# The four corners of a deformable-convolution tile: two additions of halves in one buffer instead of one strided reduction

## The reference

```
x = x + L0(gn(x))     # 7x7 neighbourhood attention
x = x + L1(gn(x))     # 3x3 convolution
x = x + L2(gn(x))     # deformable 3x3 convolution
x = x + L3(gn(x))     # two Mamba passes over the pixels
```

```
sampled = v00*(1-wy)*(1-wx) + v01*(1-wy)*wx + v10*wy*(1-wx) + v11*wy*wx
sampled = sampled * mask
out = einsum('bkhwc,ock->bohw', sampled, w2)
```

## Time and profile before

| | |
|---|---|
| two executions | 6243.54 and 6252.93 us, median 6248.24 us |
| the profiled execution | span 6244.6 us, 55481 instructions |
| from the span's start to the first gather, loading, L0 and the first image's L1 | 885.6 us |
| first gather to the last addition of `stage_flow` | 885.6 to 3134.5 us |
| rest (normalisation and Mamba) | 3134.5 to 6244.6 us |
| VectorE busy | 5012.8 us (80% of the span) |
| GpSimd busy | 4904.1 us (79%) |
| TensorE busy | 4411.3 us (71%) |

### The profile page before, as it was taken

One profiled execution on the slowest core, in us unless ns is written; L12 is line 12 of the kernel. 1 busy time (PEld: TensorE's weight loads), 2 busy tenths in 40 slices (PEclk: granted clock), 3 DMA queues, 4 the chain that ended last, 5 costly groups with the idle time before them and its releaser, 6 DMA issues. The chain is left out here.

```text
span 6244.6 us, 55481 instructions
## 1 busy us (share of the span) xinstructions
PE 4411.3 (71%) x14922; PEld 2398.8 (38%) x14922; DVE 5012.8 (80%) x3958; ACT 2533.4 (41%) x3949; POOL 4904.1 (79%) x3492
## 2 busy tenths in 40 slices
PE   3777656565555657463338888888888888888887
PEld 1566523332323233232214444444444444444443
DVE  5899736776766676666639999999999999999998
ACT  2222111111111111110026666666766766766664
POOL 1777627777777777777719999999999999999997
PEclk8887766656565656655569999999999999999999
DMA  6666623444434443443324544454454544444443
GB/s 165 133 135 136 139 79 104 123 114 145 123 104 133 127 123 105 135 116 114 104 79 149 165 157 154 161 162 148 160 163 147 169 151 156 160 153 162 155 152 120
DMA packets 379240, 855.17 MB, mean 137 GB/s; under 512 B 195672, under 2 KB 238576, under 8 KB 374580
## 3 DMA queue, kind: packets, MB, share of 16 engines
q1 hardware_dynamic: 294228, 619.96, 33.3%
q0 software_dynamic: 84672, 231.32, 12.4%
HBM read 768.83 MB, written 56.48 MB: 132 GB/s over the span
## 5 line engine op out<-in xcount | busy, mean ns | idle before, releaser
L863 POOL DMA_INDIRECT fl_quad<-table,fl_idx x1764 | 1697.3, 962 | 695.0 <-issue 536.7
L2097 POOL TENSOR_TENSOR ma_hc<-ma_h,ma_cc 128x784 f32<-128x784 f32 x1024 | 1882.2, 1848 | 235.8 <-DVE ma_h L1998 203.7
L1642 PE MATMUL ma_bank<-ma_hc,ident 128*128 128x392 f32 x4096 | 1528.0, 495 | 10.2 <-POOL ma_hc L2097 7.6
L1998 DVE TENSOR_TENSOR_SCAN ma_h<-ma_da,ma_state,ma_bank 128x784 f32<-128x784 f32 x768 | 1418.0, 1846 | 101.6 <-DVE ma_bank L1985 3.5
L1014 DVE TENSOR_TENSOR fl_part<-fl_quad,fl_bank 128x2304 f32<-128x2304 f32 x196 | 500.1, 2552 | 710.1 <-DMA fl_quad<-table,fl_idx 696.6
L1867 ACT ACTIVATE ma_da<-ma_dt,ma_a_neg 128x784 f32<-128x784 f32 x1024 | 948.2, 943 | 271.1 <-DVE ma_h L1998 176.6
L1985 DVE TENSOR_TENSOR ma_bank<-ma_dtu,ma_bank 128x784 f32<-128x784 f32 x1024 | 983.4, 960 | 80.5 <-PE ma_bank L1629 79.1
L1155 PE MATMUL fl_bank<-ident,fl_tap 128*128 128x128 f32 (+1 forms) x980 | 242.3, 409 | 937.4 <-DVE xres L1032 876.0
L1642 PEld LDWEIGHTS ma_bank<-ma_hc,ident 128*128 128x128 f32 x4096 | 705.3, 189 | 449.5 <-POOL ma_hc L2097 36.0
L1022 DVE TENSOR_REDUCE fl_tap<-fl_part 128x576 f32<-128x2304 f32 x196 | 796.5, 4064 | 0.1
L1629 PE MATMUL ma_bank<-ma_bc,ma_sel 96*128 96x512 bf16 (+1 forms) x2048 | 514.8, 333 | 376.2 <-DVE ma_h L1998 361.0
(11 more groups left out here) (229 smaller groups left out, 6131.6 us busy)
## 6 DMA issues: line engine op xcount, KB each, us to landing
ma_cc<-c_rows SPq DMA_DIRECT2D x512, 784.0 KB, 4.3
mx_win<-flat SPq DMA_DIRECT2D x64, 878.0 KB, 10.3
fl_quad<-table,fl_idx POOLq DMA_INDIRECT x1764, 2.7
table<-fl_xt SPq DMA_DIRECT2D x64, 392.0 KB
mx_mask<-in_c_mask SPq DMA_DIRECT2D x56, 294.0 KB, 4.5
ma_xs<-ma_x SPq DMA_DIRECT2D x64, 196.8 KB, 5.6
ma_xs<-ma_x SPq DMA_DIRECT2D x64, 196.5 KB, 6.1
mx_xf<-flat SPq DMA_DIRECT2D x8, 816.0 KB, 15.8
```

What stands on the lines that cost most here:

```text
L863: gp.indirect_dma_start(quad[i][:, kk, :], None, table, bass.IndirectOffsetOnAxis(ap=idx[i][:, kk:kk + 1], axis=0))\
L1642: ins = pe.matmul(ps_y[:, t, :], ident[:], hc[:, n % RH, at], start=False, stop=(n == DS - 1))
L1998: dve.tensor_tensor_scan(h[:, i % RH, :], da[:, i % RH, :], ps_bu[i % 2], before, ALU.mult, ALU.add).then_inc(scand, 1)
L2097: gp.tensor_tensor(hc[:, i % RH, :], h[:, i % RH, :], cc[:, i % (NGRP * GRP), :], ALU.mult)\
```

## The change

`part` becomes one buffer instead of two. scale(T) writes into it; it already waited for `reduced` of tile T - 1. corners(T) no longer calls one `tensor_reduce` over a strided view. It first adds the corners 2 and 3 to the corners 0 and 1, in place (2 x 576 = 1152 results), waits for a new semaphore `halved`, and then adds the two remaining halves into `tap` (576 results). The wait for `turned`, which frees `tap`, stands ahead of the second addition only.

```
-        part = [s_.sb(f"part{i}", [TS, 4, K2, CH]) for i in range(2)]
+        part = s_.sb("part", [TS, 4, K2, CH])
...
-        spread, scaled, reduced, turned, copied, projected, added, stored = (
-            s_.sem(x) for x in ("spread", "scaled", "reduced", "turned", "copied", "projected", "added", "stored"))
+        spread, scaled, halved, reduced, turned, copied, projected, added, stored = (
+            s_.sem(x) for x in ("spread", "scaled", "halved", "reduced", "turned", "copied", "projected", "added", "stored"))
...
             def scale(T):
-                e, i = T % 2, T % RQ
+                i = T % RQ
...
-                dve.tensor_tensor(part[e][:], quad[i][:].rearrange("p k (s c) -> p s k c", s=4),
+                dve.tensor_tensor(part[:], quad[i][:].rearrange("p k (s c) -> p s k c", s=4),
                                   f.unsqueeze(3).to_broadcast([TS, 4, K2, CH]), ALU.mult).then_inc(scaled, 1)
 
             def corners(T):
                 e = T % 2
                 dve.wait_ge(scaled, START + T + 1)
+                dve.tensor_tensor(part[:, 0:2], part[:, 0:2], part[:, 2:4], ALU.add).then_inc(halved, 1)
+                dve.wait_ge(halved, START + T + 1)
                 if T >= 2:
                     dve.wait_ge(turned, START + T - 1)
-                dve.tensor_reduce(tap[e][:], part[e][:].rearrange("p s k c -> p k c s"), AX_X, ALU.add)\
-                   .then_inc(reduced, 1)
+                dve.tensor_tensor(tap[e][:], part[:, 0], part[:, 1], ALU.add).then_inc(reduced, 1)
```

## The result

The changed kernel takes 6313.66 us (median of 2 runs, 6310.15 to 6317.17) against 6248.24 us: ratio 1.010, 95% interval 1.0071 to 1.013. It is slower by one percent, beyond its uncertainty and within the 2% that I called no change. The forecast was 6315 us.

What follows compares the result with a forecast made beforehand. GpSimd's gather queue was taken to bound the sampling stretch: 59 us of holds in 182 tiles, plus 9.5 in 13 late ones, less 1.9 at the end, gave +67 us, 6315 us; range 6284 to 6392 us.

Steps and rivals of the forecast that it cites:

- The bound: Sampling stretch: 1764 gathers nose to tail on GpSimd, 1.25 us each, set its 2234 us; VectorE has 3.6 us spare per tile.
- The durations: Per tile on VectorE: additions of 1.35 and 0.76 us, 0.03 us apart, replace a reduction of 4.06 us.
- The phase: In 182 tiles a gather's sensitive point falls about 1.03 us into the first addition; 13 late tiles have any phase.
- the moment: Point 0.12 us after a gather's start; a two-SBUF-input operation running then makes it wait for that operation's end, then take 0.83 us.
- The hold: First addition delays one gather per tile: 182 x 0.325 = 59 us plus 13 x 0.73 = 9.5 us; the second delays none.
- The holds there were: Gather delays already present, 28 us from prepare, corner and join: taken as zero change, within 10 us either way.
- The last tile: Only the last tile's reduction lies on the path to the stage's end, so the cheaper additions save 1.9 us there.
- Nothing held: Rival at the gathers beside the first addition: no gather is delayed, only 1.9 us saved, 6246 us; chance 0.08.
- Phase lost: Rival: the first addition's start scatters against the gathers, every tile pays 0.73 us, +140 us, 6388 us; chance 0.07.
- Both additions as one: Rival: both additions delay a gather as one, 0.79 us more per tile in phase, +221 us, 6469 us; chance 0.06.
- Dear additions: Rival: in-place addition at 1.76 ns per result, the first takes 2.03 us, +199 us, 6447 us; chance 0.02.
- VectorE as the bound: Rival: VectorE bounds the sampling stretch, so the whole 374 us come back, 5874 us; chance 0.03.

Runs made afterwards that it cites:

- the kernel with the PSUM input: Changed kernel, but the first addition adds a column of PSUM zeros instead of the other SBUF half; ScalarE's coefficient copy waits for it: 6253.81 us, ratio 0.9999.
- The long addition: Changed kernel with the first addition over 2304 results instead of 1152, into a buffer of its own: 6546.69 us, ratio 1.0474 to the kernel before.
- the kernel with two pieces: Changed kernel with the first addition cut into 816 and 336 results, a semaphore between them: 6266.57 us, ratio 1.0018 to the kernel before.
- the addition to the residual ahead: Changed kernel with the previous tile's addition to the residual moved from behind the two additions to ahead of them: 6390.68 us, ratio 1.0219 to the kernel before.
- the kernel with one buffer: Kernel before, reduction kept, with only the two product buffers made one: 6255.04 us, ratio 1.0001 to the kernel before.

## Why the prediction was right

- **The bound.** GpSimd's queue sets the sampling stretch. Shown from both sides: the kernel with the PSUM input has 379 us less work on VectorE (4633.5 us) and a ratio of 0.9999, and every kernel moved by what its gathers gained or lost, to within some 10 us. The long addition's gathers take 1996.8 us instead of 1697.3, which is +300 us, and its time lies 294.5 us above that of the kernel before.
- **The durations.** The additions take 1.357 and 0.758 us (1.355 and 0.759 by the line through two other sizes) and stand 0.04 us apart (0.03).
- **The phase.** Read in the trace of after as it was in that of before, the moment falls 0.87 us or later into the first addition in 180 tiles, 1.04 us in the mean. That was 166 of 195 before; 182 were forecast.
- **The hold.** In those 180 tiles it is 0.315 us in the mean (0.325), together 56.7 us (59). The other 15 tiles have 0.56 us in the mean, 8.3 us together (13 tiles, 9.5 us). 191 gathers are held by the first addition, none by the second.
- **The holds there were.** Taken as unchanged, within 10 us. The gathers' busy time less 1764 x 0.946 us is 28.6 us before and 96.6 after; less 65.1 by the first addition, 31.5 are left, 2.9 more. The three gathers held at the joins wait 3.07 us each now and 2.20 before, by the accident of their place, which is 2.6 us of it.
- **The last tile.** 2.0 us less (1.9).
- **A number that was off.** VectorE's wait for gathered data grew by 430 us (696.6 to 1126.4) and not by 370: the stretch itself got 68 us longer, and VectorE waits through that as well. It is on no path.
- **What was luck.** The medians lie 65 us apart and the forecast said 67, but the interval leaves 44 to 81. The terms that the trace tells apart were each right to within 3 us, and that is the reading's merit; that the two medians come out within 2 us of their sum is luck.

The rivals fall with measurements. Nothing held: the gathers' mean of 1.001 us, and the difference between the PSUM input and the SBUF input. Phase lost: 180 tiles in phase. Both additions as one: no gather held by the second. Dear additions: 1.357 us. VectorE as the bound: its waiting. What stays open is what the gather does in its 0.12 us; that it reads its indices there is inferred from what holds it. And the moment, as the prediction has it, describes operations with two SBUF inputs only: the padding also holds gathers whose moment is past (last section).

## What to carry to other kernels

Where GpSimd's gathers are the bound, VectorE's time is free and its choice of operands isn't: an operation with two inputs in SBUF, or one like the padding (one SBUF input, 0.61 ns per result), holds the gather that meets it to its end, so a slow reduction can be the better neighbour than a fast addition. Before you shorten work on an engine, see in the trace what it waits for, and what the operation that you put in its place holds up there. If such operations can't be avoided, their length and place against the gathers' rhythm set the price: the same instructions cost 65 us in one order and 135 in another, and with the first addition cut at the right point, 11.

## What the runs showed of the hardware that I had not expected

**A young operation may or may not hold.** In the kernel with two pieces, none of the 81 gathers whose moment fell 0 to 0.12 us behind the start of the second piece was held. That is no rule for all operations. With the addition to the residual ahead, five of the six additions that began 0.08 to 0.10 us ahead of a gather's moment held it to their end. And in the kernel with one buffer a join held a gather although it began 0.02 us behind the moment (2247.63 + 0.12 = 2247.75):

```profile
2247.78 3.41 DVE L878 TENSOR_TENSOR xres<-xres,fl_y 128x3136 f32<-128x3136 f32 x1
```
```profile
2247.63 4.38 POOL L863 DMA_INDIRECT fl_quad<-table,fl_idx  x1 [0.30 <-issue]
```

The joins of the kernel before began 0.05 us behind it and held nothing. The second piece waits for a semaphore of the addition right ahead of it, and the operations that held early do not; whether that makes the difference, no run tests. So the 0.12 us are good to some 0.1 us.

**The padding holds in two ways.** A gather whose padding began 0.16 us or more ahead of the gather's own start ends 0.82 us after the padding, as after an addition. But a padding that begins later than that, even after the moment, holds too, and then the gather ends 0.12 us after it. In the changed kernel:

```profile
1304.48 1.91 DVE L908 TENSOR_SCALAR fl_xp<-xres,fl_rstd,fl_nmr 64x3136 f32<-64x3136 f32 x1
```
```profile
1304.25 2.25 POOL L863 DMA_INDIRECT fl_quad<-table,fl_idx  x1 [0.30 <-issue]
```

The gather ends at 1306.50, the padding at 1306.38 (by the trace's nanoseconds). In all traces together, every padding that began up to 0.40 us after a gather's start held it, and none of those that began 0.43 us or more after it. That is why the padding's holds hardly depend on the phase: 18 to 19 us in each of the seven kernels that leave it on VectorE.

**The reduction is slow.** It takes 4.06 us for 2304 inputs, 1.76 ns for each, while an addition of 2304 results with two inputs took 2.56 us, 1.11 ns for each. Whether the stride between the corners or the operation itself makes it slow, no run tells; and yet this slowness harmed nobody here.
